# A graph network with experts on one core: the gather loop's masks read a row in PSUM, the experts are 682 columns wide

## The reference, cut to what matters

```python
x = x + _L0_gnn_ref(_layernorm(x), edge_index, ...)     # (3125, 256), 50000 edges
x = x + _L0_ffn_ref(_layernorm(x)[None], ...)[0]
x = x + _L1_gnn_ref(_layernorm(x), ...)
x = x + _L1_ffn_ref(_layernorm(x)[None], ...)[0]

# in _L0_gnn_ref: the sum over incoming edges, then four dense layers with batch norm
agg = jax.ops.segment_sum(x[src], dst, num_segments=x.shape[0])
h = (1.0 + eps) * x + agg

# in _L0_ffn_ref: 8 experts, 2 for each node, inner width 682
h1 = jnp.einsum('nc,ehc->neh', flat, w1)
h3 = jnp.einsum('nc,ehc->neh', flat, w3)
h = jax.nn.silu(h1) * h3
y = jnp.einsum('neh,ech->nec', h, w2)
out = jnp.einsum('ne,nec->nc', gates, y)
```

## Time and profile before

| what | value |
|---|---|
| runs of the kernel | 2658.03, 2651.60, 2649.38 us; median 2651.6 |
| the profiled execution | 2646.54 us; its span 2644.9 us |
| PE busy | 1871.8 us, 71% of the span |
| VectorE busy | 1496.6 us, 57% |
| GpSimd busy | 1493.3 us, 56% |
| ScalarE busy | 636.0 us, 24% |
| mean granted clock of TensorE | 0.763 of full |

### The profile page before, as it was taken

The page is one execution under the profiler, slowest core; times in us unless marked ns, Lnnn a source line. Parts: engine busy times, 40 slices in busy tenths (PEclk is TensorE's granted clock), DMA queues, the critical chain, the costliest instruction groups (busy, mean ns, idle before and its releaser), DMA issues. The chain is left out here.

```text
span 2644.9 us, 37718 instructions
## 1 busy us (share of the span) xinstructions
PE 1871.8 (71%) x9564; PEld 1346.7 (51%) x9565; DVE 1496.6 (57%) x3113; ACT 636.0 (24%) x1252; POOL 1493.3 (56%) x1583
## 2 busy tenths in 40 slices
PE   3888888876979851403999998267877777741597
PEld 2667666643434441402666665156665556530366
DVE  6555544457657561391333332547666666668698
ACT  4000000014556540161333332121111111111343
POOL 3777777725777777265663000757777777751000
PEclk8665655568989966556999999568788888865699
DMA  7333333340000050322111110331111111130100
GB/s 219 104 102 105 101 99 101 99 147 1 1 1 1 15 180 1 138 55 63 36 37 39 36 36 26 91 73 25 25 26 26 25 25 26 25 14 0 24 24 26
DMA packets 112944, 145.41 MB, mean 55 GB/s; under 512 B 46660, under 2 KB 82372, under 8 KB 112764
## 3 DMA queue, kind: packets, MB, share of 16 engines
q0 software_dynamic: 60160, 86.81, 14.0%
q1 hardware_dynamic: 52729, 57.99, 7.1%
HBM read 115.41 MB, written 29.18 MB: 55 GB/s over the span
## 5 line engine op out<-in xcount | busy, mean ns | idle before, releaser
L1445 POOL DMA_INDIRECT g<-tab_d,recs x416 | 456.3, 1097 | 149.1 <-issue 126.5
L466 PE MATMUL psA<-oh,G 128*128 128x128 f32 x1568 | 435.4, 438 | 83.7 <-DMA G<-xn_d,gat_i 34.5
L570 POOL DMA_INDIRECT rec_d<-str__1696,stp x392 | 392.8, 1002 | 174.0 <-issue 96.4
L292 POOL DMA_INDIRECT G<-xn_d,gat_i x392 | 391.9, 1000 | 144.4 <-issue 130.4
L466 PEld LDWEIGHTS psA<-oh,G 128*128 128x128 f32 x1568 | 340.8, 304 | 178.3 <-issue 83.5
L1586 PE MATMUL psS<-vv,oh 128*125 128x260 f32 x832 | 304.6, 518 | 127.9 <-DVE acc L1521 127.9
L793 PE MATMUL psZ<-z,W 128*128 (+1 forms) x1344 | 264.1, 359 | 38.9 <-DVE z L713 38.9
L1586 PEld LDWEIGHTS psS<-vv,oh 128*125 128x125 f32 x832 | 177.2, 242 | 222.2 <-DVE acc L1521 184.4
L425 DVE TENSOR_TENSOR accT<-accT,psA 128x256 f32 x392 | 165.1, 421 | 220.5 <-PE psA L466 194.5
L1197 PE MATMUL psH<-we,xh 128*128 x1344 | 238.2, 327 | 0.4 <-issue 0.3
L623 ACT ACTIVATE z<-psZ,vec 128x500 f32 (+2 forms) x112 | 70.8, 634 | 660.6 <-PE psZ L786 550.8
(11 more groups left out here) (248 smaller groups left out, 2743.2 us busy)
## 6 DMA issues: line engine op xcount, KB each, us to landing
raw<-in_L_ffn_w SPq DMA_DIRECT2D x16, 768.0 KB, 10.2
xs_d<-zero SPq DMA_DIRECT2D x1, 7168.0 KB
xs<-xs_d SPq DMA_DIRECT2D x56, 128.0 KB, 2.0
y_d<-yv POOLq DMA_DIRECT2D x56, 128.0 KB, 2.0
g<-tab_d,recs POOLq DMA_INDIRECT x416, 2.5
G<-xn_d,gat_i POOLq DMA_INDIRECT x392, 2.8
rec_d<-str__1696,stp POOLq DMA_INDIRECT x392
raw<-in_L_ffn_w SPq DMA_DIRECT2D x16, 384.0 KB, 10.6
```

The source lines that it names most:

```text
L292: pool.indirect_dma_start(out=G[:, i, :], out_offset=None, in_=xn_d, in_offset=bass.IndirectOffsetOnAxis(ap=gat_i[:, t:t + 1], axis=0)).th ...
L466: last = nc.tensor.matmul(psA[i // 2][:, i % 2, h, :], G[:, i, 128 * h:128 * (h + 1)], oh[:, i, :], start=True, stop=True)
L570: pool.indirect_dma_start(out=rec_d.rearrange("p (t r) -> (p t) r", r=2), out_offset=bass.IndirectOffsetOnAxis(ap=stp[:, h, j:j + 1], axis=0),
L1445: pool.indirect_dma_start(out=g3[:, n % BODY, j, :], out_offset=None, in_=tab_d, in_offset=bass.IndirectOffsetOnAxis(ap=recs[:, t, 1:2], a ...
```

## The change

In block 1 the row `iota` is copied once, ahead of the loop, into the PSUM tile `psT[0][1]`, whose content has been read out by then, and the one-hots compare with this copy. In block 3 the hidden width is 682: w1 and w3 are loaded and split in 682 columns (the host pads them no more), the second half of `up`, silu and the product run over 298 columns instead of 384, the last transpose of the hidden writes 42 rows, and the last chunk of `down` contracts 42 rows. The part of `psHT[1]` that the last transpose no longer writes is cleared once, and TensorE waits for that before its first tile. w2 keeps its zero rows.

```diff
+HR = 682
+HC = (HP // 2, HR - HP // 2)
+KP = [128] * (HM - 1) + [HR - (HM - 1) * 128]
...
+            iota_ps = psT[0][1][:, 0:WIN]
...
                 dve.wait_ge(s_pad, 1)
+                ch.step(nc.vector.tensor_copy(iota_ps, iota[:, :]))
                 dve.sem_inc(s_banks, TPR)
...
-                        iota[:, :].unsqueeze(1).to_broadcast([128, HT, WIN]),
+                        iota_ps.unsqueeze(1).to_broadcast([128, HT, WIN]),
...
-                sp.dma_start(raw[:, e * PIECES + 2 * j:e * PIECES + 2 * j + 2, :],
+                sp.dma_start(raw[:, e * PIECES + 2 * j:e * PIECES + 2 * j + 2, 0:HR],
...
+        s_clear = sem("s_clear")
...
+            def cols(n):
+                return HR if n % PIECES < 4 else HP
+
             def dst_half(n, s):
-                return we[:, n * PW + s * HP:n * PW + (s + 1) * HP]
+                return we[:, n * PW + s * HP:n * PW + s * HP + cols(n)]
...
-                    nc.scalar.activation(dst_half(n, 0), raw[:, n, :], ACT.Copy, scale=WS).then_inc(s_ehi, 1)
+                    nc.scalar.activation(dst_half(n, 0), raw[:, n, 0:cols(n)], ACT.Copy, scale=WS).then_inc(s_ehi, 1)
...
-                    nc.scalar.activation(sl[:, q, :], psH[q][:, :], ACT.Silu, scale=1.0 / (XS * WS)).then_inc(s_sl, 1)
+                    nc.scalar.activation(sl[:, q, 0:HC[q]], psH[q][:, 0:HC[q]], ACT.Silu, scale=1.0 / (XS * WS)).then_inc(s_sl, 1)
...
-                    nc.vector.scalar_tensor_tensor(dst_half(n, 1), raw[:, n, :], WS, dst_half(n, 0),
+                    nc.vector.scalar_tensor_tensor(dst_half(n, 1), raw[:, n, 0:cols(n)], WS, dst_half(n, 0),
...
-                    nc.vector.scalar_tensor_tensor(hv[:, i, q, :], psH[2 + q][:, :], HS / (XS * WS), sl[:, q, :],
+                    nc.vector.scalar_tensor_tensor(hv[:, i, q, 0:HC[q]], psH[2 + q][:, 0:HC[q]], HS / (XS * WS), sl[:, q, 0:HC[q]],
...
+                nc.vector.memset(psHT[1][:, 256:HP // 2], 0.0).then_inc(s_clear, 1)
                 dve.sem_inc(s_hl, 2)
...
-                            last = nc.tensor.matmul(psH[2 * w3 + q][:, :], xh[:, i, sx, 128 * k:128 * (k + 1)],
-                                                    weights(e, 2 * w3 + k, sw, q * HQ, HQ),
+                            last = nc.tensor.matmul(psH[2 * w3 + q][:, 0:HC[q]], xh[:, i, sx, 128 * k:128 * (k + 1)],
+                                                    weights(e, 2 * w3 + k, sw, q * HQ, HC[q]),
...
-                            ms = slice(128 * m, 128 * (m + 1))
-                            last = nc.tensor.transpose(psHT[q][:, ms], hv[:, i, q, ms], ident[:, :])
+                            n = KP[3 * q + m]
+                            last = nc.tensor.transpose(psHT[q][0:n, 128 * m:128 * (m + 1)], hv[:, i, q, 128 * m:128 * m + n],
+                                                       ident[:, :])
...
-                                last = nc.tensor.matmul(psY[:, :], hh[:, i, sh, 128 * m:128 * (m + 1)],
-                                                        weights(e, 4 + n, sw, (m - 3 * n) * D, D),
+                                last = nc.tensor.matmul(psY[:, :], hh[0:KP[m], i, sh, 128 * m:128 * (m + 1)],
+                                                        weights(e, 4 + n, sw, (m - 3 * n) * D, D)[0:KP[m], :],
...
+                pe.wait_ge(s_clear, 1)
                 turn(0, 0, 1)
...
         if name in ("L0_ffn_w1", "L0_ffn_w3"):
-            v = np.concatenate([v.transpose(0, 2, 1), np.zeros((X, D, HP - v.shape[1]), v.dtype)], axis=2)
+            v = np.ascontiguousarray(v.transpose(0, 2, 1))
```

## The result

| | before | changed | forecast |
|---|---|---|---|
| median of the runs, us | 2651.6 (2649.4 to 2658.0, 5 runs of this comparison) | 2635.4 (2632.1 to 2639.6, 5 runs) | 2611.8 (2600 to 2629) |
| ratio to before | | 0.9935, 95% interval 0.9918 to 0.9953 | 0.985 |
| profiled execution's span, us | 2644.9 | 2631.8 | |
| last gather of the gather loop starts | 550.3 | 537.2 | 537.5 |
| first turn of the expert tiles | 1234.1 | 1219.4 | 1218.4 |

The change is faster, by 16 us where 40 were forecast. (The forecasts in the table are the kernel before's times less the terms of the sum up to there.) The gather loop gave what the forecast said. The expert tiles gave (1645.2 - 1234.1) - (1627.0 - 1219.4) = 3.5 us of 23.9.

The account below looks back on a forecast made before the run. POOL was taken to pace the gather loop and PE to bound the expert tiles; -13.1 + 0.3 - 2.9 - 23.9 - 0.15 = -39.8 us took the median from 2651.6 to 2611.8 us, range 2600 to 2629.

Parts of the forecast that it names:

- One-hots from PSUM: Gather loop: one-hots reading PSUM no longer hold POOL's gathers; -13.1 us, bounds 0 and 14.8.
- Rival A: Gather loop: another property of the one-hot holds gathers, so only the expert part counts; 2625 us, chance 0.11.
- The copy: Ahead of the gather loop: copying iota into PSUM lies on the path; +0.3 us, bounds 0.2 and 0.5.
- The loads: Loads of w1 and w3: 682 instead of 768 columns, all but the last half-piece before the split; at nothing.
- The split: Weight split on VectorE: shorter pieces hold POOL's slot scatters less; -2.9 us, bounds 0 and 3.5.
- The expert tiles: Expert phase, PE the bound: half q=1 of the up-projection runs 298 columns instead of 384; -23.9 us.
- 56 x 0.427: Expert tiles: 12 up-projection matmuls save 36 ns each, 0.43 us per tile, over 56 tiles; -23.9 us.
- rival C: Expert tiles: PE's clock drops; a fifth of the tiles at half clock gives +68, 2680 us; chance 0.04.
- the same 0.7 us pause: PE in the expert tiles: the shorter up-projection leaves the 0.7 us pause unchanged in a shorter pair.
- both at nothing: Expert tiles: the down-projection's 42-row last chunk and the last hidden transpose stream the same columns, so neither changes the time.
- Rival B: Expert tiles: POOL or the chain of halves becomes the bound; half the 0.43 lost gives 2624 us; chance 0.11.

## Why the prediction was wrong, point by point

- **One-hots from PSUM, -13.1 forecast.** Right in cause and size: 13.1 us by the last gather, the mean gather 962 ns (forecast 0.96), the one-hot 688. In the run of this part alone it was 9.4, within the bounds: its loop restarted later, and its scans caught more gathers. That the size came out to the tenth is luck in part, for the last gather of the changed kernel starts at 537.2 to 538.8 us in five traces. Rival A falls.
- **The copy, +0.3.** The restart after it is at 55.90 us instead of 55.67. Over all traces it is mis-sized: 55.7 to 56.2 us in the six without the copy, 55.9 to 57.7 in the thirteen with it, 1 us later in the mean. The two runs of the parts alone on one chip say the same, 55.70 and 56.95.
- **The loads, 0.** Block 3 and the choice keep the 13.0 us; nothing of the loads shows.
- **The split, -2.9.** It gave 1.65 us. The casts shrank by 2.7, but one scatter more is held at the front, and every third interval keeps 1.93 us.
- **The expert tiles, -23.9.** Here the forecast failed, at two steps. The first is "56 x 0.427": the columns do save 0.43 us of PE's work in each tile, but 26 of the tiles end at a branch of the loop, where the next turn comes 3.60 us behind the first half of hh, and not behind PE's own work. 26 x 0.43 = 11.2 us went into the pause. The text even said under rival C that the shorter up-projection leaves "the same 0.7 us pause"; the pause grew. I had asked what could be late for the down-projection, and not what the 0.7 us "issue" was waiting behind. The second is "both at nothing" for the 42-row chunk: it streams the same columns, but the two changes of row count cost 0.20 us in the tile without a branch and 0.05 in the other, 27 x 0.20 + 26 x 0.05 = 6.7 us. 23.9 - 11.2 - 6.7 = 6.0, against 3.5 measured from first turn to last. The second tile, which took 6.64 us instead of 5.73, explains 0.9 of the rest; the remaining 1.6 us are not accounted for.
- **Rival B** named the size, 2624 with half of the gain lost, but not the place: neither POOL nor the chain of halves held PE in this kernel. The chain of halves set the loop's turn all the same, by its first half and through the sequencer.
- **Rival C.** The clock stayed at 0.99 in the tiles. It falls.
- **After the tiles.** 3.2 us came back in the last block's edge loop, 585.0 us instead of 581.8, and 2.4 behind it, both untouched by the change:

```profile
L1457 POOL DMA_INDIRECT g<-tab_d,recs x416 | 459.5, 1105 | 149.0 <-issue 126.5 <-DVEq L1496 22.5
```

Its gathers take 1,105 ns in the mean instead of 1,097. The same excess is in all traces of narrowed kernels on the chips without stops (459.5 to 465.3 us of gathers) and not in the two with wide experts (456.3 and 456.5). Its cause was not found; a shift of phase between gathers and VectorE is a guess that no run tests.

The version that beats both kernels is the narrowed one with 128 rows in the down-projection and the loop cut behind the first up-projection half: 2604.7 us, 47.6 less than the kernel before on its chip. It differs from the changed kernel on PE's side alone. With the new cut alone the changed kernel takes 2612.4 us. That this is close to the forecast's 2611.8 is chance: the gain comes from the loop's end, which the forecast did not price.

## What to carry to other kernels

A gap named "issue" ahead of the first instruction of a loop turn has an owner: look at the sequencer's own records, and measure from the last semaphore that really held it ahead of the branch, not from the engine's last matmul. If that distance is the same in every variant, shorter work ahead of it is worth nothing. Move the branch away from late waits, keep the register loads at it few, and count columns only in the tiles between branches. Don't narrow a contraction for its own sake: here the zero rows cost nothing, and a change of the row count between neighbouring matmuls did.

## What was not expected of the hardware

- Two changes of a matmul's row count (128 to 42 or 64, and back) cost 0.25 us together, with 0.21 us gaps in the weight loads at each; with 42 rows it is the same for one short matmul as for three.
- A loop turn on PE starts 3.60 to 3.66 us behind the release of the last wait that held PE's sequencer (18 matmuls, branch, three register loads), in 26 turns of each of five kernels. The compare and branch takes 0.22 us of it and the load of three registers 0.77.
- The load of four registers takes 0.34 and 1.0 to 1.3 us in turns, that of seven 1.1 and 1.7, and the longer one is what PE pauses for.
- Chips differ. On two of the four chips of these experiments the same kernel takes 6 to 7% longer, and its gather loop stops for some 3 us, as a rule every 17.8 us. What stops it was not found. A gain of 10 us in that loop is not to be seen there, so the parts of a change have to be compared on the kind of chip that gave its result.
